# Four graph layers on one core: row sums and the first aggregation in one stage, by blocks of 512 source nodes

## The reference, cut to what matters

```python
h = jnp.maximum(_layernorm(x, axis=-1), 0.0)
# layer 0
adj = adj + jnp.eye(N);  deg = adj.sum(axis=1);  d = deg ** (-0.5)
support = h @ W.T + b
x = x + (d[:, None] * adj * d[None, :]) @ support
# layer 1: the same form; support = h @ W.T + b is normalised over all 4096 nodes
#          (mean and standard deviation of each column) before it is aggregated
# layer 2: attention over adj != 0;  layer 3: three attention heads and two GRU cells
```

## Time and profile before

| | |
|---|---|
| time, median of 3 runs | 2142.71 us (2137.22 to 2903.79) |
| the profiled execution, its time | 2138.43 us |
| its span, first to last instruction | 2136.6 us |
| PE busy, share of the span | 88% |
| PEld / DVE / ACT busy | 56% / 79% / 68% |
| DMA, mean over the span | 229 GB/s, 489.51 MB |
| degree stage, by the timeline | 0 to 178 us |
| first aggregation, to its last product | 183 to 387 us |
| first instruction of layer 1's normalised support (L881) | 400.60 us |

### The profile page before, as it was taken

The page is one execution under the profiler, slowest core; times in us unless marked ns, Lnnn a source line. Parts: engine busy times, 40 slices in busy tenths (PEclk is TensorE's granted clock), DMA queues, the critical chain, the costliest instruction groups (busy, mean ns, idle before and its releaser), DMA issues.

```text
span 2136.6 us, 22056 instructions
## 1 busy us (share of the span) xinstructions
PE 1885.6 (88%) x7997; PEld 1199.7 (56%) x7997; DVE 1688.7 (79%) x2514; ACT 1457.4 (68%) x1529; POOL 0.8 (0%) x7
## 2 busy tenths in 40 slices
PE   2335999699988889889999969899999999999997
PEld 1224888578878888855555536544444444444443
DVE  4668999698877989887778752498889888988985
ACT  3445666456668888888787511398878788887873
POOL 0000000000000000000000000000000000000000
PEclk9999999899999999999999979999999999999999
DMA  9999999478876766668999658532342333324220
GB/s 390 429 428 361 335 344 335 181 292 316 316 273 231 244 236 237 237 231 330 345 345 360 250 214 288 188 127 95 123 128 84 128 103 109 112 104 128 94 83 10
DMA packets 81563, 489.51 MB, mean 229 GB/s; under 512 B 8449, under 2 KB 12546, under 8 KB 36402
## 3 DMA queue, kind: packets, MB, share of 16 engines
q1 hardware_dynamic: 77138, 485.94, 61.8%
q10 hardware_dynamic: 4320, 2.20, 0.3%
HBM read 452.36 MB, written 35.75 MB: 228 GB/s over the span
## 4 chain that ended last, share of the span: by engine, by line
PE 42%; DVE 9%; ACT 1%; issue 1%; DMA 0%; DVEq 0%; ACTq 0%
PE bank L1700 25%; PE bank L1662 5%; DVE work L1347 3%; PE bank L1577 2%; DVE reg L1347 1%; PE bank L1582 1%; PE bank L1583 1%; PE bank L1584 1%; PE bank L1606 1%; PE bank L1607 1%; DVE work L1325 1%; PE bank L1682 1%; PE bank L1570 1%; PE bank L1380 1%; PE bank L1609 1%
## 5 line engine op out<-in xcount | busy, mean ns | idle before, releaser
L1700 PE MATMUL bank<-work,reg 128*128 128x512 f32 x960 | 421.9, 595 | 17.3 <-DVE ring L1296 11.4
L1347 DVE TENSOR_TENSOR work<-work,ring 128x1536 f32<-128x1536 f32 x160 | 280.4, 1753 | 68.3 <-ACT work L756 67.5
L1700 PEld LDWEIGHTS bank<-work,reg 128*128 128x128 f32 x960 | 181.6, 191 | 245.9 <-issue 219.1
L934 DVE TENSOR_TENSOR a_lo<-ring,a_hi 128x2048 fp32r<-128x2048 f32 x128 | 290.8, 2288 | 31.4 <-ACT a_hi L531 30.5
L531 ACT ACTIVATE a_hi<-ring 128x2048 fp32r<-128x2048 f32 x128 | 244.2, 1912 | 76.7 <-PE bank L1505 76.7
L1537 PE MATMUL bank<-reg,ring 128*128 128x129 f32 x2048 | 245.0, 282 | 37.0 <-DVE ring L1048 37.0
L1537 PEld LDWEIGHTS bank<-reg,ring 128*128 128x128 f32 x2048 | 238.8, 197 | 42.5 <-DVE ring L1048 32.6
L756 ACT ACTIVATE work<-work 128x1536 f32<-128x1536 f32 x160 | 235.4, 1471 | 26.1 <-DVE work L1325 26.1
L1700 PE MATMUL bank<-reg 128*128 128x512 f32 x576 | 252.7, 592 | 0.0
L1503 PE MATMUL bank<-a_hi,s_hi 128*128 128x512 f32 x512 | 207.2, 405 | 20.9 <-DVE a_lo L934 20.9
L1505 PE MATMUL bank<-a_hi,s_lo 128*128 128x512 f32 x512 | 201.7, 394 | 0.0
(11 more groups left out here) (235 smaller groups left out, 2677.3 us busy)
## 6 DMA issues: line engine op xcount, KB each, us to landing
ring<-in_adj_units SPq DMA_DIRECT2D x320, 1024.0 KB, 4.9
ring<-in_adj_rows SPq DMA_DIRECT2D x32, 2048.0 KB, 17.0
ring<-masks SPq DMA_DIRECT2D x64, 512.0 KB, 4.6
masks<-work SPq DMA_DIRECT2D x48, 512.0 KB, 9.2
masks<-ring SPq DMA_DIRECT2D x16, 512.0 KB, 9.1
reg<-lines SPq DMA_DIRECT2D x8, 768.0 KB, 10.1
ring<-lines SPq DMA_DIRECT2D x8, 768.0 KB, 7.9
out<-ring ACTq DMA_DIRECT2D x8, 256.0 KB, 2.3
```

The costliest lines, as they stand in the source:

```text
L934: dve.tensor_tensor(a_lo[:, ring_at(p, g)], ring[:, ring_at(p, g)], a_hi[:, (g % 4) * UNIT:(g % 4 + 1) * UNIT].bitcast(F32), ALU.subtract) ...
L1347: dve.tensor_tensor(tv, tv, spread(ring[:, ring_at("out", g, q * W, W)], HEADS, 1), ALU.mult).then_inc(s_y, 1)
L1700: last = pe.matmul(bank[1 + k][:, :], h, tiles(c * T + t)[:, k * W:(k + 1) * W], start=t == 0, stop=t == T - 1)
```

## The change

The two stages become one. SP's loads follow one list, `STREAM`: the row halves of blocks 0 and 1 (a block is 512 sources: four row tiles, eight halves of 1 MiB), then in turn the eight units of a block, one for every destination chunk, and the row halves of the block after the next. Every entry has the slot number `n % 8` and waits for the slot's last user. For the last block the row halves are split in two fours around the units of block 6.

All eight destination chunks are summed at once, chunk `c` in `bank[c]`. A product is no longer split: 16 float32 products of 128 columns for a unit, as in layer 2, with the unit's piece as the stationary operand and the scaled support (`reg1`) as the moving one; the sum then stands with nodes on partitions and needs no transpose. Adding the identity takes four products more in each block. The split of layer 0's units on ACT and DVE is gone. Degrees are made block by block (`degrees(g)`, `degree_root(g)`), and the layer norms and projections of all eight chunks are done in the first eight row tiles, one chunk for a row tile (`support`). The node work of layer 0 for all chunks comes in the last block and behind it. The 0.75 MiB of cell weights (`gru`) are loaded later.

```diff
+STREAM = block_rows(0) + block_rows(1)
+for block in range(G - 3):
+    STREAM += block_units(block) + block_rows(block + 2)
+STREAM += block_units(G - 3) + block_rows(G - 1, 0, Q) + block_units(G - 2) + block_rows(G - 1, Q) + block_units(G - 1)
...
+            def given_back(slot, last):
+                kind, g, i = last
+                if kind == "row":
+                    sp.wait_ge(s_dega if i % 2 else s_degd, g * Q + i // 2 + 1)
+                else:
+                    sp.wait_ge(s_mm["agg0"], block_unit(g, i) + 1)
...
+            for n, (kind, g, i) in enumerate(STREAM):
+                if n >= G:
+                    given_back(n % G, STREAM[n - G])
...
+            root("deg", 0)
+            for c in range(C):
+                if c == Q:
+                    degree_root(0)
+                if c + 1 < C:
+                    root("deg", c + 1)
+                row_sum(c)
+                support_hT(c)
+                support_keep(c)
+            degree_root(1)
+            for g in range(2, G):
+                for q in range(Q):
+                    row_sum(g * Q + q)
+                degree_root(g)
...
+            def block(g, c):
+                pe.wait_ge(s_scale["agg0"], g + 1)
+                slot, count = block_slot(g, c)
+                pe.wait_ge(s_unit[slot], count)
+                for q in range(Q):
+                    for i in range(Q):
+                        o, t = bank[c][:, i * P:(i + 1) * P], g * Q + q
+                        first = slot * UNIT + q * W + i * P
+                        last = pe.matmul(o, ring[:, first:first + P],
+                                         reg1[:, t * P:(t + 1) * P], start=t == 0 and i == 0,
+                                         stop=t == T - 1 and i == Q - 1)
...
+            for c in range(C):
+                support(c)
+            for g in range(G):
+                for c in range(C):
...
+                    block(g, c)
+                    if g == G - 1 and c > 2:
+                        layer_project(c - 3)
+                    if g == G - 1 and c > 1:
+                        layer_turn(c - 2)
```

More of the change, by code:

```diff
@@ L86, in done, with block_rows, block_units @@
         assert self.n == self.k, (self.sem, self.n)
[L89 to L93, removed]
+def block_rows(g, first=0, end=2 * Q):
+    return [("row", g, i) for i in range(first, end)]
+def block_units(g):
+    return [("unit", g, c) for c in range(C)]
+STREAM = block_rows(0) + block_rows(1)
+for block in range(G - 3):
+    STREAM += block_units(block) + block_rows(block + 2)
+STREAM += block_units(G - 3) + block_rows(G - 1, 0, Q) + block_units(G - 2) + block_rows(G - 1, Q) + block_units(G - 1)
 def build(nc, x_d, rows_d, cols_d, diag_d, w_d, gru_d, col_d, row_d, masks_d, lines_d, out_d):
@@ L312, in build, with block_unit, row_slot, block_slot @@
                 arrival[p, n] = landed[n % SLOTS[p]]
+        def block_unit(g, c):
+            return g * C + c
+        def row_slot(t, half):
+            return STREAM.index(("row", t // Q, 2 * (t % Q) + half)) % G
+        def block_slot(g, c):
+            n = STREAM.index(("unit", g, c))
+            return n % G, 16 * sum(kind == "unit" for kind, _, _ in STREAM[n % G:n + 1:G])
         def loaded(p, c, g):
@@ new lines, in _ @@
+            for c in range(C):
+                s = Steps(dve, s_ln["deg"], LN_STEPS["deg"], c)
+                norm_in(s, c)
+                if c:
+                    dve.wait_ge(s_hturn["deg"], c)
+                s.inc(norm_out(s, "deg", c, c + 1))
+                s.done()
+                row_sum(c)
+                if c == 0:
+                    constants()
+                if c == Q:
+                    degrees(0)
+            degrees(1)
+            for g in range(2, G):
+                for q in range(Q):
+                    row_sum(g * Q + q)
+                degrees(g)
@@ L1408, in project @@
                 pe.wait_ge(s_hT[p], c)
[L1409 to L1420 removed]
+                if p == "agg1":
                     pe.wait_ge(s_pkeep["agg0"], C)
@@ L1438, in project, with support @@
                 last.then_inc(s_proj[p], 1)
[L1441 to L1449 removed]
+            def support(c):
+                pe.wait_ge(s_ln["deg"], (c + 1) * LN_STEPS["deg"])
+                if c:
+                    pe.wait_ge(s_hT["deg"], c)
+                turn(bank[6], hn).then_inc(s_hturn["deg"], 1)
+                pe.wait_ge(s_hT["deg"], c + 1)
+                if c:
+                    pe.wait_ge(s_pkeep["deg"], c)
+                for q in range(Q):
+                    o = bank[7][:, q * P:(q + 1) * P]
+                    pe.matmul(o, ones[0:1, :], rows[0:1, 0:P], start=True, stop=False)
+                    last = pe.matmul(o, hT[:, q * P:(q + 1) * P], w0t, start=False, stop=True)
+                last.then_inc(s_proj["deg"], 1)
```

368 lines of the change are left out of this document (193 added, 175 removed).

## The result

The changed kernel takes 2147.7 us (median of 14 runs, 2144.3 to 2150.0) against 2141.2 for the kernel before (14 runs). The ratio is 1.0033, with a 95% interval from 1.0025 to 1.0042: no change by the 2% bound, and a real loss of 0.3%. The forecast was 2148, so the total came out as said. One of the 14 runs of the kernel before took 2903.8 us, a slow run that the ratio leaves out; the other 13 lie between 2136.5 and 2142.7.

The account below looks back on a forecast made before the run. ACT's loop was to bound the start (102 us), DMA the 39.7 us rounds, PE the end (398.0); a 12 us tail put the marker at 410.0, 9.4 later: 2138.4 + 9.4 = 2148 us, range 2122 to 2186 (forecast alone 2135 to 2165).

Parts of the forecast that it names:

- The start: First loop: ACT's serial chain of 9.6 us a chunk, then block 0's degrees, lets PE start block 0 at 102 us.
- The block on PE: Block products: 0.112 us each, 3.57 us a unit, 28.6 us for eight units plus 0.9 for the identity.
- Rival B: Block products: a unit costs PE 3.83 us, giving 2163 us, or 2201 at 4.41; chance 12%.
- The low clock: PE after each wait for loads: starts at half clock, losing 2.3 us a round (bounds 1.8 and 3.5).
- The turn: Between blocks: the next block's first unit queues behind the eighth row half, leaving PE idle 7.7 us.
- The rounds: Time per block: DMA's 16 loads of 2.48 us take 39.7, PE's round 39.5; 39.7 was taken.
- Rival C: Mixed row and unit loads: DMA falls to 372 GB/s, rounds take 45.1 us, total 2180 us; chance 10%.
- The dense end and the tail: Blocks 6 and 7 take 29.5 us each plus node work, ending at 398.0; 12 us later the marker, 410.0.
- The sum: Whole kernel: marker 9.4 us later, at 410.0, added to the profiled 2138.4 us gives 2148 us.
- A: First loop: PE's clock is up, a projection costs some 3.3 us instead of 5.9, total 2127 us; chance 12%.
- D: Blocks: PE stays at the lower clock throughout, 64 x 3.6 us more, some 2340 us; chance 4%.
- E: Whole load stream: it never stops, marker near 352, total 2090 us; needs ACT's loop at 4.9 a chunk; chance 5%.

Follow-up runs that it names:

- e5_filler: Changed kernel plus 29 zero products on PE ahead of each of blocks 1 to 5, to keep its clock up: 2145.35 us, ratio 1.0032.
- e4_half_products: Changed kernel with half of the block products left out, all loads and row sums kept: 2132.3 us in its one run.
- e7_turns: Changed kernel with bias added on DVE, projection copy after the next row sum, and units and row halves loaded alternately in blocks 0 to 5: 2113.1 us, ratio 0.9883.
- e8_one_ahead: Changed kernel with bias added on DVE, projection copy after the next row sum, and rows loaded one block ahead, alternating with units: 2109.8 us, ratio 0.9868.
- e2_bias_out: Changed kernel with the bias of layer 0's projection moved from PE products to one DVE addition a block: 2118.2 us, ratio 0.9897.

## Why the prediction was right, point by point

**The start, mechanism right, the term too long.** The working said 102; it was 94.4. It was made of the end of the first projection (30.5, measured 28.5), seven chunks of 9.6 (measured 9.02, so 4.1 us less) and a degree chain of 4 (measured 2.8). The step that failed is the sum of a chunk from durations: the row sum is in the rows at 1.90 us, and the next instruction of ACT starts 1.80 after it; the kept projection lasts 0.60 and is followed after 0.50. Added durations of neighbours on an engine count such overlaps twice. Start-to-start differences would have given 9.0. In the first projection's term two things are off. From 18.9 the working's own items (2.29, 1.4, 1.6) make 24.2 and not 21.8; the 21.8 holds only if DVE starts on the first half of the tile, one load of 2.45 us earlier, which the working doesn't say. And the changed kernel's DVE started at 15.18 and needed 4.9 us for the three, so that ACT's second root came at 20.11.

**The block on PE, right.** 0.112 us between products, 3.57 a unit; PE's busy time in a round was 31.1 to 31.8; the forecast has 31.8, of which 2.3 for the low clock. Block 3's 152 products in a run of 17.14 us give (17.14 - 0.28) / 151 = 0.112. The page's busy time, 243.3 us, is layer 2's 245.0 again, but the forecast's reading, start to start, is the one that holds. Rival B falls.

**The low clock, right and without weight.** The granted clock was 0.87 to 0.89 in rounds with a wait of 9 us, so about a quarter of each round, waits included, went at the lower level (1.2 GHz): (1 - 0.88) / 0.5. Block 3 shows the price: its first 104 products took 13.97 us, and at 0.112 they would take 11.8. With most of the low stretch taken out, the time didn't change (`e5_filler`). The Trainium skill (TensorE: Matmul & The Clock Gate, section on HAM oscillation) speaks of kernels that lose by such waits; the trace agrees that the clock falls in them, and the filler shows that here it was no loss.

**The turn, right in place, its wait longer.** Five waits, one ahead of each of blocks 1 to 5, of 8.0 to 9.5 us against 7.7. The forecast took the wait from PE's side, one lone load and a second. But DMA still had row halves in its queue then: ahead of block 4 the first unit went out at 247.27 us and needed 8.8 to land, against 4.8 for a lone one. So the wait is what DMA's round leaves over: 40.7 less 31.5. This changed no total, since the forecast took the longer of the two rounds.

**The rounds, 1 us short.** (297.4 - 134.7) / 4 = 40.7 against 39.7. The loads keep a share of 1.00 to 1.01 but move 410 to 417 GB/s in three of the four; two rounds took 41.2. Part of it shows at the turns. In the last 10 us ahead of block 4 the loads moved 371 GB/s, and ahead of block 5 398, against 419 to 423 in the 10 us before each. The queue of loads is short there, since PE gives back a slot only every 3.57 us and a load takes 2.48: row halves landed from 5.9 us after their issue on, and SP holds back some of the next units until row halves are summed (8.2 us of waits around the turn ahead of block 4). In `e4_half_products`, `e7_turns` and `e8_one_ahead` no load of the full rounds landed in under 14.3 us, and their rounds moved 420 to 422. The short queue may be the reason, but it isn't shown: ahead of block 2, with row halves that landed from 6.7 us on, the rate was 425. The rest is open: in these three kernels too one round each was 1.2 to 1.5 us long, at the full rate. Rival C in its own size, 372 GB/s, falls. The Trainium skill (DMA: Bandwidth & Descriptors, Specifications) names 358 GB/s as a core's share; by the trace one core alone moved 423 in block 1.

**The dense end and the tail, right.** Blocks 5, 6 and 7 took 97.1 us from block 5's start (working: 97.7), and the tail 11.0 (12 forecast, 13.4 before).

**The sum.** The start was 7.6 us too long; the five rounds 4.7 too short; the end and tail together 1.6 too long. The marker came at 405.5 instead of 410.0, and of the missing 4.5 us the profiled execution lost about 4 behind it. The forecast also started from the profiled execution, 2138.4, which lies 2.8 below the median of the 14 runs. From there the measured shift of 4.9 makes 2143, from the median 2146. So three things cancel in the 2148: a base 2.8 too low, a shift 4.5 too large, and the 1.6 behind the marker that stay open. The sum's closeness is luck; that the change costs a few us, and through which stages, is not.

**The rivals.** None came: A not (no projection at full clock in the changed kernel), nor B, C, D or E. E's condition, a chunk at 4.9 us, needs the bias out of the projection, and the loop then ran at 5.4 a chunk. `e8_one_ahead` reached 2110, 2090 being the forecast's limit of the loads alone. Two prices don't follow from their own numbers. For A, 5.9 us times 0.39 / 0.63 is 3.7 and not 3.3 (the two levels as measured in `e2_bias_out`, 1.16 against 2.07, do give 3.3). For D, 64 x 3.6 on top of 2148 is 2378 and not 2340. Neither touches the forecast.

## What to carry to other kernels

When two stages with different limits are merged, price first the loop that feeds the merged one: work that was hidden under loads (here a projection of 5.9 us and its place in ACT's order) becomes the path, and it can cost as much as the merge brings. Here four bias products a chunk cost 27 us at the marker. An edit that gives 0.0% in one kernel can give over 1% in its successor, so measure again what was once found to be hidden. Where both sides' rounds are nearly equal, try the loads of both streams in turn rather than in lumps: here it took the long waits away and brought 2.6 us at the marker, too little for the times to tell. The list with the rows one block ahead brought 3.8 more.

## What the runs showed of the hardware

- Fp32 products with one row of weights between products with 128 rows are dear: 0.72 us for each, bias or product, at the lower clock, against 0.52 when all are of one kind (5.86 against 2.07 us for the chunk). The edit also did away with the second product into the same output; which of the two makes the price, no run here separates.
- A wait of 9 us on PE is followed by a low stretch of the clock (0.55 in the first 5 us of block 3); waits of 1.2 us between units of 3.8 us are not (granted clock 1.00 in `e7_turns` and `e8_one_ahead`). A single wait of 2.4 to 2.5 us was followed by 0.66 over 4.6 us in `e8_one_ahead`, and by no fall in `e7_turns`.
- An instruction's recorded length reaches past the start of the next one: by about 0.1 us on ACT, and by more on PE, where 2048 products with a mean of 283 ns fill 243.3 us.
- In the first 94 us the granted clock reads 1.00 although the projections ran at the lower level. Their own lengths tell the level, not that column.
- One core alone held 420 to 428 GB/s as long as its queue was long (14 us and more from issue to landing in the rounds of `e7_turns`), and moved 371, 398 and 408 in the last 10 us ahead of three blocks of the changed kernel, where loads landed from 5.9 us on. Ahead of block 2 it was 425, so no run here settles the reason.
